# Counting of edges in a graph kernel: the per-edge codes are fixed ahead, VectorE takes over GpSimd's part, and the batch counts are read from a table of one number per node span

## The reference

```python
def spmm(feat):                       # layer 0, ten times
    msg = feat[col] * w[:, None]
    return jax.ops.segment_sum(msg, row, num_segments=n)
...
def _gcn_conv(x, W, b, src, dst, norm, n):      # layer 3, twice
    h = x @ W
    msg = h[src] * norm[:, None]
    out = jax.ops.segment_sum(msg, dst, num_segments=n)
    return out + b
...
dst = jnp.minimum((3125 * jax.random.uniform(key, (100000,)) ** 2.0).astype(jnp.int32), 99999)
_o = jnp.argsort(dst, stable=True)    # the edges come sorted by dst; low nodes have many more
```

## Time and profile before

| | |
|---|---|
| median of three runs | 2815.78 us (2812.81 to 2824.91) |
| the profiled execution: time, span | 2801.42 us, 2799.7 us |
| mean granted TensorE clock over the span | 0.735 of full |
| busy over the span: TensorE, VectorE, ScalarE, GpSimd | 1853.1, 1564.5, 861.7, 936.1 us |
| VectorE in `count_edges`: `hot_w` and `hot_p`, 300 of each | 297.0 and 127.3 us |
| TensorE's count matmuls, 1196 | 287.6 us |

### The profile page before, as it was taken

How to read it: one execution, slowest core, us unless ns; L and a number is a source line. 1 busy time by engine, 2 the same in 40 slices (tenths; PEclk the granted TensorE clock), 3 DMA queues, 4 the chain that set the end, 5 groups by cost and what they waited for, 6 DMA issues and landing times. The chain is left out here.

```text
span 2799.7 us, 50246 instructions
## 1 busy us (share of the span) xinstructions
PE 1853.1 (66%) x14611; PEld 1446.8 (52%) x14611; DVE 1564.5 (56%) x4031; ACT 861.7 (31%) x1484; POOL 936.1 (33%) x1182
## 2 busy tenths in 40 slices
PE   1777777779999999778525544544555555555488
PEld 0333444459999999745413433333444344333477
DVE  7856866665444444465434555555555555555753
ACT  1687566641111111121212222222222222222420
POOL 3311211131000000000166666666666666666100
PEclk9988988879999999889755555555555555555699
DMA  4211111110000000800132222222222222222200
GB/s 138 93 49 41 42 70 56 70 63 2 2 2 2 2 2 2 311 1 3 37 44 49 49 49 48 47 49 48 50 50 49 49 50 49 49 48 48 69 1 18
DMA packets 86652, 133.19 MB, mean 48 GB/s; under 512 B 48616, under 2 KB 55656, under 8 KB 86462
## 3 DMA queue, kind: packets, MB, share of 16 engines
q1 hardware_dynamic: 40398, 83.53, 8.8%
q0 software_dynamic: 25344, 38.98, 6.9%
q10 hardware_dynamic: 20720, 8.06, 1.3%
HBM read 95.89 MB, written 34.58 MB: 47 GB/s over the span
## 5 line engine op out<-in xcount | busy, mean ns | idle before, releaser
L1430 POOL DMA_INDIRECT counts<-p_rows,rows x784 | 745.6, 951 | 498.4 <-issue 224.0
L931 PE MATMUL ps_hop<-y,counts 128*128 128x192 f16 x6250 | 525.0, 247 | 21.6 <-DVEq L818 12.3
L1659 PE MATMUL ps_e_z<-e_w_q,counts 128*128 128x96 f32 x1568 | 364.1, 427 | 259.8 <-ACT counts L1595 219.9
L931 PEld LDWEIGHTS ps_hop<-y,counts 128*128 128x128 f16 x6250 | 520.0, 98 | 26.5 <-DVEq L818 12.4
L1659 PEld LDWEIGHTS ps_e_z<-e_w_q,counts 128*128 128x128 f32 x1568 | 341.8, 330 | 295.8 <-ACT counts L1595 249.9
L560 DVE TENSOR_TENSOR hot_w<-iota_w,places_now 128x1600 f16<-128x1600 f16 x300 | 297.0, 990 | 156.0 <-PE ps_counts L586 137.1
L586 PE MATMUL ps_counts<-hot_w,hot_p 128*128 x1196 | 287.6, 372 | 117.5 <-DVE hot_p L560 77.4
L1670 PE MATMUL ps_e_seg<-counts 128*128 128x192 f16 x784 | 140.7, 359 | 301.9 <-DVE counts L1470 151.1
L1670 PEld LDWEIGHTS ps_e_seg<-counts 128*128 128x128 f16 x784 | 100.4, 138 | 385.3 <-issue 198.2
L1595 ACT ACTIVATE counts<-ps_e_u 96x1024 f32<-96x1024 f32 x98 | 99.9, 1019 | 642.0 <-remote 591.1
L527 POOL TENSOR_TENSOR places_now<-places,origins (+1 forms) x302 | 115.4, 383 | 428.0 <-DVE hot_p L560 278.3
(11 more groups left out here) (401 smaller groups left out, 2483.4 us busy)
## 6 DMA issues: line engine op xcount, KB each, us to landing
counts<-count_rows SPq DMA_DIRECT2D x30, 800.0 KB, 6.6
count_rows<-attr_split SPq DMA_DIRECT2D x25, 800.0 KB, 3.8
counts<-p_rows,rows POOLq DMA_INDIRECT x784
e_attr<-attr_parts SPq DMA_DIRECT2D x99, 72.0 KB
attr_parts<-attr_split SPq DMA_DIRECT2D x9, 784.0 KB, 15.9
attr<-attr_parts SPq DMA_DIRECT2D x50, 140.6 KB
e_dst_rows<-dst_row SPq DMA_DIRECT2D x99, 64.0 KB
e_w_q<-q_rows ACTq DMA_DIRECT2D x392, 12.0 KB
```

Source lines behind the costliest of these rows:

```text
L931: mm = pe.matmul(ps[:, r, 0:2 * D], k.counts[:, m, b, :], y[:, odd, b, :], start=b == 0, stop=b == NB - 1)
L1430: nc.gpsimd.indirect_dma_start(z[:, slot, j, :], None, k.p_rows, bass.IndirectOffsetOnAxis(rows, 0)) \
L1659: mm = pe.matmul(ps_z[:, two, j // (STEP_TILES // 2), at:at + D], u_hot[:, two, j * P:(j + 1) * P], w_q[:, fed, j // Q_TILES, :], start=Tr ...
```

## The change

- **Codes.** `setup` writes for each edge two fp16 codes (each twice, side by side), so that a window needs no subtraction: VectorE compares `codes` with a slice of one long ramp `iota_c` (3,200 numbers, made by GpSimd) that starts where the block or the window does. `places`, `places_now`, `origins` and `iota_w` are gone, and so is GpSimd's loop.
- **VectorE's loop** is now one loop per window, 200 of them written out, with `hot_p` made ahead of `hot_w`. Each batch computes its tile number, its bounds check and its three addresses in registers. Each window loads one number.
- **The table** holds one number per window: the batches in it and its first tile. Engines add the batches up in registers as they go. The sum over windows that TensorE made in `setup` (`ps_base`) is gone.
- **The edge-feature buffer** `attr` lies in `attr_split`'s unused rest, so its memset on GpSimd waits for the stores from there.

```diff
-            nc.vector.tensor_copy(k.places[:, 0:TILES, 0], src_i[:, :])
-            step(nc.vector.tensor_scalar(dst_i[:, :], dst_i[:, :], 4, None, ALU.arith_shift_right))
-            nc.vector.scalar_tensor_tensor(k.places[:, 0:TILES, 1], dst_i[:, :], float(APART), part_f[:, :], ALU.mult, ALU.add)
+            nc.vector.tensor_scalar(part_i[:, 0, :], dst_i[:, :], 4, WINDOWS - 1, ALU.arith_shift_right, ALU.bitwise_and)
+            step(nc.vector.tensor_scalar(dst_i[:, :], dst_i[:, :], NOWHERE - (P - 1), None, ALU.bitwise_and))
+            nc.vector.memset(k.codes[:, TILES:, :, :], NO_PLACE)
+            nc.vector.scalar_tensor_tensor(k.codes[:, 0:TILES, 1, :], twice(part_i[:, 0, :]), float(WIDE),
+                                           twice(part_f[:, :]), ALU.mult, ALU.add)
+            nc.vector.scalar_tensor_tensor(k.codes[:, 0:TILES, 0, :], twice(dst_i[:, :]), -float(FIRST), twice(src_i[:, :]),
+                                           ALU.add, ALU.add)
...
-            nc.vector.tensor_copy(ends[:, 5, :], whole[:, 1, :]).then_inc(counted, 1)
-            dve.wait_ge(counted, 2)
+            nc.vector.tensor_copy(cols[:, 1, :], ends[:, 2, :])
+            nc.vector.tensor_copy(cols[:, 0, :], whole[:, 1, :]).then_inc(cols_made, 1)
+            dve.wait_ge(row_made, 1)
+            step(nc.vector.tensor_copy(row[:, :], ps_row[:, 0:2 * NW]))
+            step(nc.vector.scalar_tensor_tensor(k.window_tabs[:, :], row[:, NW:2 * NW], float(BY_TILE), row[:, 0:NW],
+                                                ALU.mult, ALU.add))
...
-        def last_of(eng, w):
-
-            return eng.value_load(k.window_tabs[0:1, bass.ds(w + 1, 1)])
+        def window_of(eng, w):
+
+            word = eng.value_load(k.window_tabs[0:1, w:w + 1])
+            return word & (BY_TILE - 1), word >> 10
...
         @block.gpsimd
         def _(pool):
-            pool.sem_inc(places_ready, 2)
-
+            nc.gpsimd.memset(zeros[:, :], 0.0).then_inc(zeros_set, 1)
+            pool.wait_ge(k.parts_stored, 16 * 9)
             nc.gpsimd.memset(attr[:, :], 1.0).then_inc(ones_set, 1)
...
-            with dve.Fori(0, (last + 4) >> 2) as four:
-                for q in range(4):
-                    s = q % 2
-                    dve.wait_ge(places_ready, four * 4 + (q + 3))
-
-                    dve.wait_ge(hot_used, four * 4 + (q + 1))
-                    for hot, n, c in ((hot_w, WIDE, 1), (hot_p, P, 0)):
+            first = 0
+            for w in range(NW):
+                d, j = w // WINDOWS, w % WINDOWS
+                n, tile_of_first = window_of(dve, w)
+                end = dve.snap(first + n)
+                shift = dve.snap(first * BATCH - tile_of_first)
+                with dve.Fori(first, end) as i:
+                    tile = i * BATCH - shift
+
+                    dve.wait_ge(hot_used, i + 1)
+                    for hot, lo, n, c in ((hot_p, d * P, P, 0), (hot_w, j * WIDE, WIDE, 1)):
                         made = nc.vector.tensor_tensor(
-                            hot[:, s, :, :].rearrange("p j (e t) -> p j e t", t=2),
-                            iota_w[:, 0:n].rearrange("p (e t) -> p e t", t=2).unsqueeze(1)
+                            hot[:, bass.ds(i & (HOTS - 1), 1), :, :].rearrange("p a j (e t) -> p (a j) e t", t=2),
+                            k.iota_c[:, lo:lo + n].rearrange("p (e t) -> p e t", t=2).unsqueeze(1)
                             .broadcast_to([P, BATCH, n // 2, 2]),
-                            now[:, q, :, c, :].unsqueeze(2).broadcast_to([P, BATCH, n // 2, 2]), ALU.is_equal)
+                            k.codes[:, bass.ds(tile, BATCH), c, :].unsqueeze(2).broadcast_to([P, BATCH, n // 2, 2]),
+                            ALU.is_equal)
                     made.then_inc(hot_ready, 1)
+                first = end
...
-                done, last = last_of(pe, d * WINDOWS - 1), last_of(pe, d * WINDOWS)
                 for j in range(WINDOWS):
-                    after = last_of(pe, d * WINDOWS + (j + 1)) if j < WINDOWS - 1 else None
-                    window(d, j, done, last)
-                    done, last = last, after
+                    following = d * WINDOWS + j + 1
+                    ahead = pe.snap(end + window_of(pe, following)[0]) if following < NW else None
+                    window(d, j, first, end)
+                    first, end = end, ahead
```

More of the change, by code:

```diff
@@ L37 @@
 WIDE = NB * WIN
+CODES = NB * P
+NO_PLACE = 2047.0
 BATCH = 4
+BY_TILE = 1024
+HOTS = 2
 U_PARTS = 4
@@ L193, in setup @@
         tile_id = sb("tile_id", [P, 3, TROWS], F32)
-        ends = sb("ends", [HALF_W, 7, 2], F32)
+        ends = sb("ends", [HALF_W, 5, 2], F32)
+        row = sb("row", [1, 2 * NW], F32)
         whole = sb("whole", [HALF_W, 2, 2], I32)
@@ L580, in open_bank, with window @@
                                  skip_group_check=True)
-            def window(d, j, done, last):
-                with pe.Fori(done + 1, last + 1) as i:
-                    pe.wait_ge(hot_ready, i + 5)
+            def window(d, j, first, end):
+                with pe.Fori(first, end) as i:
+                    pe.wait_ge(hot_ready, i + 1)
                     for t in range(BATCH):
                         mm = pe.matmul(ps[:, j % 2, 0:WIDE],
-                                       hot_p[:, bass.ds(i & 1, 1), t, :].rearrange("p a s -> p (a s)"),
-                                       hot_w[:, bass.ds(i & 1, 1), t, :].rearrange("p a s -> p (a s)"),
+                                       hot_p[:, bass.ds(i & (HOTS - 1), 1), t, :].rearrange("p a s -> p (a s)"),
+                                       hot_w[:, bass.ds(i & (HOTS - 1), 1), t, :].rearrange("p a s -> p (a s)"),
                                        start=False, stop=False, skip_group_check=True)
@@ L631, in one_block @@
                             edges(n)
+                return first, end
             open_bank(0, 0)
+            first, end = 0, pe.snap(window_of(pe, 0)[0])
             for d in range(NB):
-                one_block(d, d % 2)
+                first, end = one_block(d, d % 2, first, end)
             pe.wait_ge(window_out, NW + 2)
-            pe.sem_inc(hot_used, 2)
             for n in range(len(PARTS)):
```

79 lines of the change are left out of this document (18 added, 61 removed).

## The result

The changed kernel takes 2918.4 us (median of 4 runs, 2903.3 to 2926.3), the kernel before 2814.3 us beside it (2811.3 to 2824.9): ratio 1.036, 95% interval 1.031 to 1.041. It is slower, as forecast, but by 104 us and not by 42, and it lies above the range. The profiled execution has a span of 2901.6 us against 2799.7 us, so 101.9 us more.

What follows compares the result with a forecast made beforehand. VectorE's sequencer was expected to become VectorE's bound in the counting, with ScalarE still setting blocks 1 to 4. Terms 6 + 0 + 14 + 15 + 6 + 1 = +42 us on 2815.8 gave 2858 us, range 2812 to 2893.

Steps and rivals of the forecast that it cites:

- the hiding registers: Rival: in the counting, VectorE's register instructions stay hidden under the comparisons; 2816 us, 2 in 10.
- the freed TensorE: Rival: in the counting, TensorE sheds a load per block and VectorE's waits for GpSimd go; 2796 us, 1 in 10.
- The memset: GpSimd's later memset of attr costs nothing, since SyncE issues until 86.8 us; uncovered, 1.8 us once.
- The setup: Setup: larger code operations and one table operation more, less the dropped exchange with TensorE; +1 us.
- Code loading: Rival: VectorE's 3,000 more instructions wait 1.2 us per 250, 14 waits adding 16 us; 2874 us, 1 in 10.
- 1.5 + 128 x 2.05 = 263.9 against 248.5: Blocks 9 to 24: VectorE's register time for 129 batches in 128 windows against the measured stretch; +15 us.
- 101.6 against 88: Blocks 5 to 8: VectorE's register time for 56 batches in 32 windows against the measured stretch; +14 us.
- 121 us, under the 139 that ScalarE sets. 0: Blocks 1 to 4: VectorE's register time stays below the stretch bound by ScalarE's edge features; 0 us.
- the coupling's 6: TensorE and VectorE at nearly equal pace with two buffers lose 0.3 us in each of 20 blocks; +6 us.
- Block 0: VectorE's registers take 71.9 us instead of 57, from an earlier start near 52.8; ends at 129 against 123, +6 us.
- TensorE's registers: Late blocks: two more per batch end, one per window start, taking TensorE's pace from 13.4 to some 15.2 us.
- The stages behind should be the same to the microsecond: All stages after the counting, which the change leaves alone, keep their times; 0 us.

Runs made afterwards that it cites:

- dve_extra: bounded plus sixteen ALU operations and three small address groups per batch in VectorE's loop; ratio 1.0251 to the kernel before.
- no_check: Changed kernel with each batch's tile number declared within the list, so VectorE makes no bounds check; ratio 1.0249 to the kernel before.
- lean_all: Changed kernel without the bounds check, with window limits in registers on TensorE and limits and tile number in registers on VectorE; ratio 1.0037 to the kernel before.
- lean: Changed kernel with TensorE's window limits kept in three registers, two ALU operations fewer per batch; ratio 1.0318 to the kernel before.
- bounded: Kernel before with table entries holding a window's last batch plus one, masked to ten bits after each load; ratio 1.0119 to the kernel before.
- lean_no_check: Changed kernel with both the edit of lean and that of no_check; ratio 1.0113 to the kernel before.
- pairs: lean_all with attr in its own tile and one table word for two windows' counts on TensorE; ratio 0.9939 to the kernel before.
- after_again: Changed kernel run again unaltered, on a chip of the group with shorter stages behind the hops; ratio 1.0362 to the kernel before.
- pairs_hint2: pairs plus a branch hint at the end of TensorE's loop over the hops; ratio 0.9878 to the kernel before.

## Why the prediction was wrong in size

**What held.** The mechanism: VectorE's sequencer became its bound and the loads ran under the comparisons. A window's first batch takes 2.00 us (predicted 2.05), a batch in a window 1.62 to 1.66 (1.5), together 559 us (558). That the two sums agree so closely is luck: 99 batches at 0.12 us too little make 12 us, and 200 first batches at 0.05 us too much give back 10. The group with the check takes 371 to 386 ns where I had put 235, and an ALU operation 45 to 53 where I had put 40; the gaps are somewhat shorter, and a window's load with what goes with it comes to 0.38 us, not 0.55. The direction was right in block 0 and from block 5 on, and it was right to give the hiding registers and the freed TensorE low chances. The memset was rightly put at nothing; the swap of the two comparisons wasn't tried by itself.

Three slips of the working changed little. The setup was put at +1 and the counting's block starts 2.5 us later; and that lateness stands in the sum twice, once in the start at 52.8 us and once as a term of its own. Code loading with 3,000 more instructions and a wait for each 250 gives 12 waits, not 14. And the operation at 1500.95 us under which a load ran is an addition, not a comparison, which leaves the reading as it is.

**The step that failed** is the one from price to stretch: "1.5 + 128 x 2.05 = 263.9 against 248.5", "101.6 against 88", and "121 us, under the 139 that ScalarE sets. 0". On the right of each stands a measured stretch, with all its stalls in it; on the left a product with none. The stalls don't go away when one engine gets slower: 42 us of waits for TensorE, 12 us of slow loads and 12 us of gaps in the code came on top of the 559, and the prediction had room for 28 of these 65 us (4 us of waits in block 0, the coupling's 6, and 18 of slack that its sum left in blocks 1 to 4). The 37 us beyond are nearly all of the 41 by which the counting was missed. The late blocks show it best. Undisturbed blocks before and after, and blocks with a low granted clock, each with its length (columns as in the earlier trace rows):
```profile
428.30:443.00 14.70, 10.15 (x94) 6.04 (x94) 9.87 (x16) 10.32 (x17) 1.49 (x7) 1.00 0.19 67
443.00:460.20 17.20, 14.02 (x94) 7.74 (x94) 11.77 (x19) 10.38 (x17) 2.67 (x9) 0.70 0.15 57
```
```profile
470.10:486.90 16.80, 12.05 (x94) 6.55 (x94) 10.62 (x16) 10.67 (x17) 0.00 (x0) 0.90 0.16 59
486.90:505.80 18.90, 15.55 (x94) 7.99 (x94) 10.62 (x16) 10.61 (x17) 0.00 (x0) 0.64 0.16 54
```
Before, a block takes 14.7 us or, where TensorE's clock is low, 17.2; after, 16.8 or 18.9. The right sum sets like against like: 16.8 less 14.7 is 2.1 us for each of 16 blocks, 34 us, and 32.7 were measured; of the blocks 10 to 24 three are of the low kind before and four after, about as many. I had set 16.4 against the mean of both kinds, 15.5.

**Blocks 1 to 4** were put at 0, since ScalarE sets their pace. It is busy 118 of 148 us now and 117 of 139 before, so it never set it alone: 18 us of VectorE's waits for TensorE lie there, and slack of 18 us (139 less 121) on one of three engines that wait for each other isn't free. dve_extra makes 5.3 us here out of VectorE's registers alone, and no_check and lean_all take 2.7 and 5.5 us back. How much is TensorE's clock, which with the same matmuls kept it busy 10.5 us longer (0.80 against 0.86), isn't taken apart.

**Block 0** was put at 129 and ends at 140.4. Of the missing 11 us 2 are registers (73.9 against 71.9), 6 are waits for TensorE above the 4 allowed (its first eight matmuls take 2.84 us at 56.4 us, and four take 0.85 us from 68 us on), 1.6 are a slow load and a gap, and 1.1 is the later start.

**TensorE's registers** were put at some 15.2 us for a late block, just under VectorE's 16.4. lean confirms that they are hidden there, and bounded shows that in the old form 0.16 us a window of them, with GpSimd's 0.04 beside it, cost 25 us. Taking VectorE's away alone (no_check) gives little in the late blocks for that reason: an undisturbed one takes 16.3 us there, and 14.9 once TensorE's are gone too (lean_no_check).

**"The stages behind should be the same to the microsecond"** failed by 20 us. 12.7 are the position of TensorE's code, shown in both forms. Here the rival of code loading was right that the place of code costs time, and wrong about where: VectorE's new code, which I had suspected, shows 28 gaps of 0.4 us, 12 us, whose cause no run tried, while TensorE's unchanged loop lost 13. The Trainium skill has the background in "Runtime: NRT & Kernel Launch", section "Instruction fetch mechanics": code comes in blocks of 256 instructions, fetched ahead in sequence, and a taken branch to a block that isn't there waits for the fetch. The hops agree with that: the gaps follow the jump back, and the next end of a block where the head was put so that one lies some 25 instructions behind it, and stand at no other hop. No run shows the fetch itself. The Trainium skill says there too that crossing from one block to the next is mostly hidden; the rest of each hop agrees, with no gap over 0.4 us, and the place seven or eight matmuls behind a jump doesn't, with 1.2 to 2.4 us in the runs that have the gap.

**Left open.** The 7.5 us in the stages behind the hops. In one group of chips these take 1416.1 to 1418.6 us in all nine kernels, old form and new, and 1627.0 to 1630.7 in the four of the other group; so the 1637.1 us of the profiled execution look like its own, but I have no second profile of the changed kernel from that group. What lowers the clock in some late blocks and not in others wasn't tried by itself, and it is worth more than some of the edits: a low block costs 2 to 3 us, and their number among the blocks 10 to 24 goes from one (pairs) to nine (bounded, lean and lean_all). Less register work on TensorE doesn't by itself raise the clock: lean has 0.80 in the late stretch, after_again beside it 0.80 too.

## What to carry to other kernels

When two engines take turns and both are near the bound, to price a change on one of them, compare undisturbed periods with undisturbed periods, and add the stalls afterwards to both sides. Registers count as work on the sequencer that sets the pace: the group with the bounds check took 0.39 us a batch and a table load 0.30 us a window, about as long as `hot_p` with 0.43; on a sequencer that has time they cost nothing, as lean shows. Here the cheap cure (running registers, a declared bound, two counts in one word, a branch hint) turned a kernel that was 3.6% slower into one that is 1.2% faster than before. And when stages that nobody touched move, look for gaps on "issue" behind a loop's jump back before looking for anything else.

## What the hardware showed that I hadn't expected

- A fused register group isn't one price: in VectorE's loop 47 to 57 ns for the small ones, 99 for the one ahead of `hot_w`, 386 for the one that holds the bounds compares and 275 for the same group without them (no_check). On TensorE some 0.06 us stand between two register instructions, on VectorE 0.03 to 0.05.
- A register load takes 0.30 us, but 0.54 to 0.93 us on VectorE about once a block, in the windows after a store of `count_rows` was issued.
- VectorE's straight code of 19 instructions a window has a gap of 0.38 to 0.40 us every seventh window.
- The same loop of 1,250 matmuls and 1,250 weight loads takes 534, 547 or 520 us (five rounds of it), by where its head lies and by a hint at its end.
- The same count matmuls ran at quite different granted clocks in the late stretch: 0.80 in lean, 0.83 in the changed kernel, 0.95 in pairs and 0.98 in pairs_hint2. A block at a low clock takes 2 to 3 us more.
